# Weight preparation moved into the first block's turn, and an own order of dense groups for the second turn

## What is computed

```
x1  = x + (attention(layernorm(x)) @ Wo + bo)     # 16 heads of 32, causal, softmax
x2  = layernorm(x1)
out = x1 + shared(x2) + experts(x2)
shared(x2)  = (silu(x2 @ shared_gate.T) * (x2 @ shared_up.T)) @ shared_down.T
experts(x2) = 32 experts, 4 per token (best 3 of 8 groups), capacity 320 slots each
```

## Time and profile before

| | us |
|---|---|
| median of three runs | 2515.92 (2512.40 to 2517.86) |
| the profiled execution, its own time | 2496.56 |
| its span in the profile | 2494.5 |
| granted TensorE clock, mean share of full speed | 0.972 |
| busy: PE, DVE, ACT, POOL | 2295.1, 1570.9, 1079.4, 1105.4 |

### The profile page before, as it was taken

How to read it: one execution, slowest core, us unless ns; L and a number is a source line. 1 busy time by engine, 2 the same in 40 slices (tenths; PEclk the granted TensorE clock), 3 DMA queues, 4 the chain that set the end, 5 groups by cost and what they waited for, 6 DMA issues and landing times. The chain is left out here.

```text
span 2494.5 us, 48721 instructions
## 1 busy us (share of the span) xinstructions
PE 2295.1 (92%) x15466; PEld 1153.5 (46%) x15466; DVE 1570.9 (63%) x4870; ACT 1079.4 (43%) x1849; POOL 1105.4 (44%) x1622
## 2 busy tenths in 40 slices
PE   3788999999999999999999999999998886999997
PEld 1334444444444444444444444444444343666664
DVE  4355666675766666666666666666666654666664
ACT  3344444444444434343434443434342314666664
POOL 1223234434343434444444434444443534677775
PEclk8899999999999999999999999999999997999999
DMA  4212122222222222222222222222212016888885
GB/s 167 69 43 60 47 74 55 70 58 71 53 71 63 65 67 59 72 66 61 61 61 61 60 60 61 60 60 60 61 43 77 22 43 195 233 237 234 235 235 118
DMA packets 180850, 222.52 MB, mean 89 GB/s; under 512 B 37776, under 2 KB 119792, under 8 KB 180624
## 3 DMA queue, kind: packets, MB, share of 16 engines
q1 hardware_dynamic: 154000, 177.58, 24.1%
q0 software_dynamic: 26624, 42.12, 7.7%
HBM read 112.65 MB, written 56.46 MB: 68 GB/s over the span
## 5 line engine op out<-in xcount | busy, mean ns | idle before, releaser
L936 DVE CUSTOM_DVE_ANT_0 junk<-scores,maskrow 128x512 f16<-128x512 f32 (+3 forms) x1024 | 461.5, 487 | 188.9 <-PE scores L543 111.0
L669 ACT ACTIVATE probs<-scores_T 128x512 f32<-128x512 f32 x640 | 367.1, 598 | 193.6 <-PE scores_T L558 190.8
L1054 POOL TENSOR_SCALAR_AFFINE_SELECT probs<-probs 128x256 f32<-128x256 f32 x512 | 192.0, 412 | 334.5 <-ACT probs L669 334.0
L1063 POOL DMA_INDIRECT slots_dram<-rec,idx x256 | 257.7, 1007 | 120.6 <-issue 80.1
L558 PE MATMUL scores_T<-stack_q,stack_k 97*128 97x512 f16 (+3 forms) x1024 | 248.7, 305 | 49.1 <-ACT probs L669 35.9
L543 PE MATMUL scores<-stack_k,stack_q 96*128 96x512 f16 (+3 forms) x1024 | 250.4, 306 | 46.0 <-DVE nmax L936 42.7
L1040 POOL TENSOR_TENSOR xres<-xres,bo 128x512 f32<-128x512 f32 x64 | 81.2, 1271 | 264.7 <-DMA xres<-in_x 264.7
L191 PE MATMUL dense<-xT_hi,wqkv_hi 128*128 128x512 f16 x512 | 196.8, 384 | 1.5 <-DVE xT_lo L907 1.5
L192 PE MATMUL dense<-xT_lo,wqkv_hi 128*128 128x512 f16 x512 | 195.6, 382 | 0.0
L193 PE MATMUL dense<-xT_hi,wqkv_lo 128*128 128x512 f16 x512 | 195.5, 382 | 0.0
L1182 POOL DMA_INDIRECT out<-ex_y,ex_sidx x96 | 152.6, 1589 | 77.9 <-issue 40.0
(11 more groups left out here) (229 smaller groups left out, 5502.2 us busy)
## 6 DMA issues: line engine op xcount, KB each, us to landing
stack_q<-split_q SPq DMA_DIRECT2D x384, 64.0 KB, 2.0
stack_k<-split_k SPq DMA_DIRECT2D x384, 64.0 KB, 2.0
out<-xres SPq DMA_DIRECT2D x67, 256.0 KB, 3.1
xres<-in_x SPq DMA_DIRECT2D x64, 256.0 KB, 2.9
x2n_dram<-x2n SPq DMA_DIRECT2D x16, 1024.0 KB, 4.3
ex_raw_wg<-in_W_gate SPq DMA_DIRECT2D x32, 512.0 KB, 4.1
ex_raw_wu<-in_W_up SPq DMA_DIRECT2D x32, 512.0 KB, 5.1
ex_raw_wd<-in_W_down SPq DMA_DIRECT2D x32, 512.0 KB, 8.6
```

Source lines behind the costliest of these rows:

```text
L669: act.activation(to, at, ACT.Exp, scale=SCALE / (QS * QS)).then_inc(exp_done, 1)
L936: last = dve.tensor_tensor_reduce(out=c["junk"][:, f % 2, at:at + cols], in0=ps["scores"][f % 2][:, at:at + cols], in1=c["maskrow"][:, SEQ ...
L1054: last = pool.affine_select(out=blk, in_=blk, compare_op=ALU.is_ge, fill=0.0, base=0, pattern=[[0, 2], [1, P]], channel_multiplier=-1)
L1063: pool.indirect_dma_start(out=a["slots"], out_offset=bass.IndirectOffsetOnAxis(ap=c["idx"][:, t, k:k + 1], axis=0), in_=c["rec"][:, t, k, ...
```

## The change

- `setup` keeps the constants, the load of x of block 0 (now four DMAs, one per tile of 128 tokens), the q/k bias, and the loads of the three parts of `Wqkv`. Nothing is split there, and ACT and PE have no work in it. SP doesn't wait for any load in it.
- SP issues the loads of Wo, shared_up, shared_down, the router weight, the biases, the tables' DMAs (which it waits for) and then shared_gate at the start of `sequences`, ahead of turn 0.
- ACT splits the q weight between its second and third norm of block 0, the k and v weights after the transposes' copies. DVE's parts follow in the same order. The other five go into turn 0: ACT at slots 12, 22, 32, 42, 66 (Wo, shared_up, shared_down, router, shared_gate), DVE one slot later.
- The value bias: spread by DVE at slot 70, multiplied by PE at slot 80, added at slot 84. DVE's memset of row 96 becomes four of 2048 elements at slots 100, 104, 108, 112.
- In turn 0 SP loads the next x ahead of the first stacks, not after them.
- New waits: PE's q, k, v of block 0 on their splits, S_T of block 0 on the four memsets, some others that guard reused memory.
- Turn 1 gets its own list `GROUPS_1` (plan `PLAN_1`).

```diff
+GROUPS_1 = ([g for m in range(HG) for w in ("q", "k") for g in ((w, m, 4), ("none", 0, 4))]
+            + [g for t in range(TT) for g in (("v", t, 4), ("none", 0, 5))] + [("none", 0, 9)] + [("xT", t, 1) for t in range(TT)])
...
+PLAN_1 = Plan(GROUPS_1, 126, 3, 1, {})
...
+            for t in range(TT):
+                sp.dma_start(c["xin"][:, t, :], x_v[0][:, t, :]).then_inc(begin["x0_loaded"][t], 16)
+            sp.dma_start(c["bqk"][:, :], a["bqkT"]).then_inc(begin["bias_loaded"], 16)
+            for n in range(3):
+                sp.dma_start(c["raw"][n], weight_of(a, n)).then_inc(begin["raw_loaded"][n], 16)
...
-            dve.memset(c["stack_k"][SROWS:SROWS + 1, :, :, :], MS)
...
+SPLIT_ORDER = (0, 1, 2, WO, SU, SD, RW, SG)
+SPLIT_SLOT = {slot: place for place, slot in zip(range(3, 8), (12, 22, 32, 42, 66))}
+
+BV_SPREAD, BV_PRODUCT, BV_ADDED = 70, 80, 84
+ROW_SLOT = {100 + 4 * hg: hg for hg in range(HG)}
...
+            load_raw(WO)
+            load_raw(SU)
+            load_raw(SD)
+            load_raw(RW)
...
+            sp.wait_ge(tables_written, 16 * (1 + 2 * CS))
+            load_raw(SG)
             turns(sp, turn)
...
+                if kind in WEIGHT and in_first(s) and m == 0 and k == 0:
+                    pe.wait_ge(weight_lo, split_place(WEIGHT[kind]))
...
+            norm1(0, 0)
+            norm1(0, 1)
+            weights_hi(0)
+            norm1(0, 2)
+            norm1(0, 3)
             for t in range(TT):
                 copies(0, 0, [("xT", t, 0, 1, t % DENSE, 0)])
+            weights_hi(1)
+            weights_hi(2)
             turns(act, turn)
...
+            def first_steps(slot):
+                if slot - 1 in SPLIT_SLOT:
+                    weights_lo(SPLIT_SLOT[slot - 1])
+                if slot == BV_SPREAD:
+
+                    dve.wait_ge(direct_loaded, 16 * 3)
+                    for k in range(DK):
+                        dve.tensor_scalar_mul(spread[:, k, :], c["ones"][:, :], c["bvT"][:, k:k + 1]).then_inc(bv_spread, 1)
+                if slot == BV_ADDED:
+                    dve.wait_ge(bv_done, 1)
+                    dve.tensor_tensor(c["bo"][:, :], c["bo"][:, :], ps["o"][:, :], ALU.add).then_inc(bo_ready, 1)
+                if slot in ROW_SLOT:
+                    dve.memset(c["stack_k"][SROWS:SROWS + 1, ROW_SLOT[slot], :, :], MS).then_inc(rows_made, 1)
...
             for t in range(TT):
                 statistics1(0, t)
+            dve.wait_ge(begin["bias_loaded"], 16)
+            dve.tensor_scalar_mul(c["bqk"][:, :], c["bqk"][:, :], QS).then_inc(bias_scaled, 1)
+            weights_lo(0)
             for t in range(TT):
                 copies(0, [("xT", t, 0, 1, t % DENSE, 0)])
+            weights_lo(1)
+            weights_lo(2)
```

More of the change, by code:

```diff
@@ L199, in need, with setup @@
         eng.wait_ge(sem, count)
-def setup(nc, a, c, ps):
+def setup(nc, a, c, begin):
     with ExitStack() as ctx:
         sem = lambda n: ctx.enter_context(nc.semaphore(n))
[L205 to L209, removed]
-        block = ctx.enter_context(nc.Block())
[L213 to L219, removed]
+        zeroed, made = sem("setup_zeroed"), sem("setup_made")
+        block = ctx.enter_context(nc.Block())
@@ L232, in _ @@
[L232 to L241, removed]
@@ L260, in _ @@
             pool.iota(c["fill_i"], pattern=[[P, CS], [1, P]], base=TOKENS, channel_multiplier=0).then_inc(made, 1)
-            pool.memset(c["ones"][:, :], 1.0).then_inc(ones_made, 1)
+            pool.memset(c["ones"][:, :], 1.0)
             pool.memset(c["half"][:, :], -0.5)
@@ L281, in _ @@
[L281 to L303, removed]
@@ L340, in sequences @@
         dve_chain, settled = sem("dve_chain"), sem("settled")
+        weight_hi, weight_lo, bias_scaled = sem("weight_hi"), sem("weight_lo"), sem("bias_scaled")
+        tables_written, direct_loaded = sem("tables_written"), sem("direct_loaded")
+        bv_spread, bv_done, bo_ready, rows_made = sem("bv_spread"), sem("bv_done"), sem("bo_ready"), sem("rows_made")
+        raw_loaded = begin["raw_loaded"]
+        split = [both(c["wqkv"], ALL, ALL, slice(n * D, (n + 1) * D)) for n in range(3)]
+        split += [both(c[n], ALL, ALL, ALL) for n in ("wo", "sgT", "suT", "sdT", "rwT")]
+        spread = c["att"][:, :].rearrange("p (k m) -> p k m", k=DK)
         block = ctx.enter_context(nc.Block())
@@ L426, in stack, with stacks, load_next @@
                                  c["split_" + name][part][h * HD:(h + 1) * HD, groups, :]).then_inc(stacked[half], 16)
+            def stacks(i):
+                stack_ready(i, 0)
+                for name in ("q", "k"):
+                    for n in range(3):
+                        stack(name, n, 0)
+            def load_next(i, fin):
+                b = i - 2
+                sp.wait_ge(done["xT"], (i + 1) * TT)
+                settle(sp)
+                if fin:
+                    sp.wait_ge(x2n_stored, (b + 1) * 16)
+                    settle(sp)
+                for t in range(TT):
+                    if fin:
+                        sp.wait_ge(done["x2T"], b * TT + t + 1)
+                        settle(sp)
+                    sp.dma_start(c["xin"][:, t, :], x_v[i + 1][:, t, :]).then_inc(xin_loaded[t], 16)
             def turn(i, par, proj, attn, fin, nxt):
@@ L436, in turn @@
                     place_maxima(i - 1, 2)
[L437 to L441, removed]
-                if nxt:
[L443 to L452, removed]
+                if proj and not in_first(i):
+                    stacks(i)
+                if nxt:
+                    load_next(i, fin)
+                if in_first(i):
+                    stacks(i)
                 if attn:
@@ L480, in _, with value_bias @@
             ident = c["ident"][:, :]
+            WEIGHT = {"q": 0, "k": 1, "v": 2, "out": WO, "router": RW, "gate": SG, "up": SU, "down": SD}
+            def value_bias():
+                pe.wait_ge(bv_spread, DK)
+                pe.wait_ge(raw_loaded[WO], 16)
+                for k in range(DK):
+                    last = pe.matmul(ps["o"][:, :], spread[:, k, :], c["raw"][WO][:, k, :], start=k == 0, stop=k == DK - 1)
+                last.then_inc(bv_done, 1)
             def dense(i, slot, groups, before):
@@ L600, in turn @@
                     dense(i, slot, groups, before)
+                    if in_first(i) and slot == BV_PRODUCT:
+                        value_bias()
             first = before_turn(0)
@@ L681, in turn @@
                         exp(i - 1, *EXP_SLOT[slot])
+                    if in_first(i) and slot in SPLIT_SLOT:
+                        weights_hi(SPLIT_SLOT[slot])
                     copies(par, slot, groups)
@@ L690, in turn, with weights_hi @@
                         att_hi(i - 1, AHI_SLOT[slot])
-            for t in range(TT):
-                norm1(0, t)
+            def weights_hi(place):
+                n = SPLIT_ORDER[place]
+                act.wait_ge(raw_loaded[n], 16)
+                act.activation(split[n][0], c["raw"][n], ACT.Copy, scale=WS).then_inc(weight_hi, 1)
+            norm1(0, 0)
[3 more added lines that the diff above has]
+            norm1(0, 3)
             for t in range(TT):
                 copies(0, 0, [("xT", t, 0, 1, t % DENSE, 0)])
+            weights_hi(1)
+            weights_hi(2)
             turns(act, turn)
@@ L1351, in transformer_block @@
             c = {"ident": ident}
+            begin = {"bias_loaded": first.enter_context(nc.semaphore("bias_loaded"))}
+            for n, count in (("x0_loaded", TT), ("raw_loaded", 8)):
+                begin[n] = [first.enter_context(nc.semaphore(f"{n}{t}")) for t in range(count)]
             def pair(name, shape):
```

95 lines of the change are left out of this document (67 added, 28 removed).

## The result

| | before | after |
|---|---|---|
| median, us (6 runs each) | 2513.18 (2509.82 to 2517.86) | 2495.82 (2488.41 to 2499.92) |
| ratio after to before, 95% interval | | 0.9909 (0.9890 to 0.9928) |
| span of the profiled execution | 2494.5 | 2494.0 |

The change saves 0.9%: 17.4 us between the medians, 22.9 us by the ratio, against a forecast of 26.5. The two profiled spans are almost equal, which fits none of these. So I compare the start by marks: the first S_T of turn 1 and that of turn 2 (before's are in the earlier trace rows).

A forecast was written before the change was run, and what follows sets the result against it. PE bounds the kernel from turn 2 on, so savings at the start go through to the end. 19.5 us to the first S_T plus 7 in turn 1 gave 26.5: 2515.9 to 2489.4 us, range 2474 to 2503 (chance 0.8).

The forecast's parts named there:

- the first rival: Turn 1's new list only trades waits: gain there 0 to 2, total 19 to 21, 2496 us; chance 0.20.
- Start of the norm and splits in it: Block 0: statistics start at 6.3 (bounds 6.0 to 7.5); q split costs 0.8, projections start at 18.7.
- Projections, not held: Block 0's projections: 34.0 us, 18.7 to 52.7, no PE wait, 1.1 to 1.4 us to spare in the banks.
- Bias product: Turn 0, slot 80: PE idles 3.3 us, then the product takes 5.54 (bounds 3.5 and 6.8).
- Memsets: DVE, maxima of block 0: four of 1.72 us cost 4.7 net (bounds 2.0 and 6.9); first S_T at 86.1.
- absorbed 2.2 us: The second and third memsets fall into DVE's 1.33 and 0.86 us waits for xT_hi, taking 2.2 off their cost.
- Turn 1: With the new list, first to last S_T takes 79.4 us against 86.5: gain 7 (bounds -2 and 14).
- hold behind slot 85: Late turn 1: S_T waits 7.5 us on the next block's norm and ACT's exponentials; the new list leaves this unchanged.
- Short memsets and a clock that stays up: Rival: 2.7 from memsets, 2 from the product, up to 14 in turn 1; gain 33 to 38, 2480; chance 0.12.
- Code loading: Rival: instruction pages wait behind weight loads at 6 to 30, 14.4 us each; one page or late SP 0.06, slower 0.04.
- three signs of being wrong: First S_T later than 95, instruction packets before 60, or turn 1 not shorter than 98.
- SP held nothing up: Answers the rival that SP, waiting for tables, starts turn 0's stacks late (after 62, not 36); one page or late SP 0.06.

The follow-up runs named there:

- run 2: Kernel before with only turn 1's new list added: turn 1 took 94.3 us, ratio to before 0.9977.
- run 9: Changed kernel with shared_gate's split at slot 46 in place of 66: first S_T at 82.36, ratio to before 0.9883.
- Run 4: Changed kernel with the four memsets at slots 50, 53, 56, 59 in place of 100 to 112: first S_T at 78.90, ratio to before 0.9878.
- run 5: Changed kernel with bias spread, product and sum at slots 46, 56, 62 in place of 70, 80, 84: ratio to before 0.9901.
- run 6: Changed kernel with both the memsets early (slots 50 to 59) and the bias product early (slot 56): first S_T at 78.09, ratio to before 0.9869.
- run 7: Changed kernel with memsets and bias product early, plus turn 1's v groups moved: turn 1 took 89.5 us, ratio to before 0.9852.
- run 10: Changed kernel with memsets, bias product and shared_gate split early and v groups moved: 2478.86 us against before's 2518.49, ratio 0.9837.

## Why the prediction was right, and where its sizes were off

The time lies in the range and on the side forecast, and the mechanism was the one named: an earlier start, less the product and the memsets that come onto the path, and a shorter turn 1. Three sizes in it were off (product, memsets, turn 1). The trace is 20.9 us ahead at turn 2 (20.1 by the means of two traces of each), against a sum of 26.5. The number alone would have misled: 2495.82 is what the first rival forecast (2496, no gain from the list), yet the list did gain and what was missing was mostly lost at the start.

- **Start of the norm and splits in it.** Forecast 6.3 and 18.7, measured 6.22 and 18.55. The second is sound: the q split cost 0.7 where I had 0.8. The first is in part luck. I had let SP's eight issues end last, at about 5.4; they ended at 4.70, and what the barrier waited for was DVE's casts, which ended at 5.92 and which I hadn't counted:

```profile
4.19 0.51 SPq L220 DMA_DIRECT2D probs<-in_Wqkv  x1
...
5.23 0.69 DVE L254 CAST xres<-xres 32x384 f32<-32x384 int32 x1
...
6.22 0.69 DVE L770 BATCH_NORM_STATS2 stats<-x2n 128x6 f32<-128x512 f32 x1 [0.30 <-PEq L208]
```

- **Projections, not held.** 34.05 us. The copy of q1 started at 31.4 (32.1 forecast) and PE had no wait. The slack in the banks held, although two of POOL's splits grew from 1.16 to 2.51 and 2.68 us.
- **Bias product.** The gap was 3.01 (3.3). The product was mis-sized: 5.54 was taken from the earlier trace rows, where the clock rose on the way (weight loads 0.85 us apart, then 0.43); the same product in the setup took 6.64 in the second trace of before and 6.22 in run 2, so one row was thin ground. Here it was 6.71, near the upper bound of 6.8. Without the gap it was 3.60 (run 9). I had named the gap as a cost of 3.3 and not that it can nearly double what comes behind it.
- **Memsets.** Forecast 4.7, measured 6.8: from the start of the second fill to the end of the cast 18.9 us pass in the changed kernel (66.42 to 85.34), 12.2 before (89.81 in the earlier trace rows to 101.97). The casts, changed kernel and before:

```profile
85.16 0.18 DVE L1001 CAST nmT<-nmF 128x32 f16<-128x32 f32 x1
```

```profile
101.79 0.18 DVE L945 CAST nmT<-nmF 128x32 f16<-128x32 f32 x1
```

  The absorbed 2.2 us were right: four rows of 1.76 with the 0.48 that DVE is shown idle ahead of each make 9.0, and 9.0 less 2.2 is 6.8. The price of one was wrong, and here I had gone by the row alone. The Trainium skill (VectorE: DVE Perf Modes, Zero memsets can be issued as uint32) says one cycle per element; at the page's 0.96 GHz that is an estimate of 2.13 us for 2048 elements. Run 4 agrees: memsets in a row started 2.13 apart, of which the row shows 1.76 and 0.37 to 0.38 is "issue" in front. My test of the rule on the earlier trace rows couldn't decide, since 2.58 us of "issue" stand ahead of that memset's row too. By the rule the term would have been 6.3, still 0.5 short.
- **Turn 1.** 7 forecast, 4.4 measured. The first quarters were 24.7 and 22.3 (25.3 and 22.5 forecast, though 20.3 and two waits of 1.0 make 22.3), with the waits of 1.03 to 1.05 behind the copies of q and k groups where I had put 1.0. The third, to the end of the denominators, was 21.6 for 19.0: the wait for the mask was 2.44, and behind it the product with v ran mostly at 1.2 GHz, 4.05 for the 2.36 at full clock. The last stretch was 13.9 for 12.6 to the last S_T, and the second stacks and maxima then took 12.5 us, where before took 12.8. The hold behind slot 85 was there, as forecast.

The shares of the miss: 0.8 us at the second fill, where the product's 1.2 us more met a start 0.15 earlier and a shorter gap; 2.1 the memsets; 0.2 the placing of the maxima; 2.6 turn 1. But for rounding that is the 5.6 us between 26.5 and 20.9.

**The rivals.** The new list does more than trade waits (run 2: 4.9 us), though less than I forecast. Short memsets and a clock that stays up are out: 6.8 us and 6.71. Code loading: an instruction packet before 60 us was one of my three signs of being wrong, and it came, between 35 and 36 us of the changed kernel, when the loads of shared_gate and x were just ending. The queue's line for 30 to 40 us:

```profile
q8 instruction: 1, 0.02, 0.7%
```

PE had no wait from 18.55 to 52.49, so the sign was a bad one: this packet cost nothing. Between 5 and 34 us, while the weights were loading, none came in any of the nine traces with the new start, so what one would have cost there no run shows. SP issued its first stacks at 36.44, when POOL's split of k1 (35.20 and 1.16) had ended, and its last of these by 59.6, far ahead of the first S_T at 89.20. So SP held nothing up.

## What to carry to other kernels

Moving work from a serial setup under a full engine paid here in full at first, 30.6 us at the first projection. But look at what then stands at the seam between two stages: of those 30.6 us 16.4 were left at the first S_T (105.64 to 89.20). The rest, 14.2, is 9.6 of a wait and of a product that ran at the low clock behind it, and 4.6 of the next stretch (27.0 for 22.4), where four small memsets stood on the engine that bounds it. Moved some slots earlier, into DVE's idle time, the memsets cost nothing that shows (run 4: 12.3 us against the 12.2 of before), and the product without a gap takes 3.6. Where PE waits, give the work behind the wait its length at the low clock as the upper bound; here it came out anywhere from 3.70 to 6.75. And compare traces by marks near the change: the spans of these two differed by 0.5 us, with 20.9 us of gain at turn 2.

## What the runs showed of the hardware

- **The clock behind a gap.** The same eight fp32 matmuls took 3.60 us with no gap ahead (runs 5, 6, 7, 9 and 10), and 3.70, 5.09, 6.71 and 6.75 behind a gap of 3.01 us; granted clock 1.00 in run 5 and 0.55 in the stretch of the last. A wait of 1.17 us with sparse work ahead of it was followed by the low clock in one trace of the old list (4.49 us for the product with v) and by the full one in the two traces of before (2.36). Behind a wait of 2.44 to 2.45 us the same product took 4.05 in three traces of the new list and 2.36 in four.
- **A memset holds DVE longer than its row says.** 1.76 us in the row, 2.13 to 2.14 from start to start for 2048 elements. Only this length was issued several times in a row, so the runs don't show whether the missing 0.37 grows with the length (2.13 us would be 1.04 ns an element) or is a fixed piece of each.
- **DVE and POOL beside each other.** DVE's split of shared_down took 2.86 us in place of 2.29, and that of the router 1.11 in place of 0.29, while POOL's splits took 2.51 and 2.68 in place of 1.16. These rows of the changed kernel overlap, and the last line is the router's split before:

```profile
35.64 2.86 DVE L1086 SCALAR_TENSOR_TENSOR sdT_lo<-stack_k,sdT_hi 128x2048 f16<-128x2048 f32 x1 [1.42 <-ACT sdT_hi L739]
38.55 1.11 DVE L1086 SCALAR_TENSOR_TENSOR rwT_lo<-denT,rwT_hi 128x128 f16<-128x128 f32 x1
```

```profile
36.84 2.68 POOL L1130 TENSOR_TENSOR split_q<-glu,split_q 128x512 f16<-128x512 f32 x1 [0.49 <-ACT split_q L661]
```

```profile
29.75 0.29 DVE L280 SCALAR_TENSOR_TENSOR rwT_lo<-denT,rwT_hi 128x128 f16<-128x128 f32 x1
```

The Trainium skill (Advanced Engine Details and Errata, GPSIMD Details) says that POOL shares a read and a write interface with DVE and conflicts with DVE instructions that have two inputs in SBUF, as these have. The rows agree. I had priced the splits as if alone; under PE's 34 us it cost nothing. It isn't only instructions with two inputs: moved early, beside POOL's splits, the spread of the bias, whose only tensor input is `ones`, took 2.66 us in place of 0.87 (run 5), while POOL's split next to it took 1.20:

```profile
38.92 1.20 POOL L1130 TENSOR_TENSOR split_k<-glu,split_k 128x512 f16<-128x512 f32 x1
39.03 2.66 DVE L1066 TENSOR_SCALAR att<-ones,bvT 128x128 f32<-128x128 f32 x4
```
